# Second layer norm applied by ScalarE, the attention output's remainders by GpSimd, and all engines' orders set anew

## What is computed

```python
x = x + attention(layernorm(x), Wq, Wk, Wv, Wo)
x = x + moe(layernorm(x), ...)
# attention: 16 heads of 16, q and k through elu + 1, causal running sums
kv_sum += k_i (outer) v_i;  k_sum += k_i
out_i = (q_i @ kv_sum) / (q_i . k_sum + 1e-8);  result = out @ Wo.T
# moe: sigmoid router over 8 experts in 4 groups, the best 2 groups,
# the best 4 experts, weights normalised and times 2.5; plus a shared expert
y = sum_e cw_e * ((silu(x @ Wg_e) * (x @ Wu_e)) @ Wd_e)
layernorm(x) = (x - mean) / sqrt(var + 1e-5)
```

## Time and profile before

| what | us |
|---|---|
| median of 3 timed runs | 1055.8 (1051.72 to 1056.35) |
| the profiled execution | 1048.01 |
| its span, first to last instruction | 1046.2 |
| TensorE busy | 978.1 |
| VectorE busy | 832.0 |
| GpSimd busy | 529.2 |
| ScalarE busy | 459.9 |

### The profile page before, as it was taken

The page is one execution under the profiler, slowest core; times in us unless marked ns, Lnnn a source line. Parts: engine busy times, 40 slices in busy tenths (PEclk is TensorE's granted clock), DMA queues, the critical chain, the costliest instruction groups (busy, mean ns, idle before and its releaser), DMA issues. The chain is left out here.

```text
span 1046.2 us, 34557 instructions
## 1 busy us (share of the span) xinstructions
PE 978.1 (93%) x14749; PEld 838.1 (80%) x14749; DVE 832.0 (80%) x1751; ACT 459.9 (44%) x856; POOL 529.2 (51%) x432
## 2 busy tenths in 40 slices
...
GB/s 224 4 21 44 82 64 150 111 84 154 25 174 87 107 133 53 160 70 146 100 68 159 51 175 86 133 106 64 152 67 148 113 77 154 41 149 43 142 76 46
DMA packets 262457, 105.71 MB, mean 101 GB/s; under 512 B 175648, under 2 KB 244768, under 8 KB 262304
## 3 DMA queue, kind: packets, MB, share of 16 engines
...
## 5 line engine op out<-in xcount | busy, mean ns | idle before, releaser
L766 POOL TENSOR_TENSOR et<-et,cw_all 128x512 f32<-128x512 f32 x124 | 162.1, 1315 | 278.9 <-DMA cw_all<-cw_dram 179.8
L1025 PE MATMUL bank<-xt_hi,wg_hi 128*128 128x512 f32 x576 | 238.0, 413 | 11.4 <-DVE compare L880 7.9
L1025 PE MATMUL bank<-xt_lo,wg_hi 128*128 128x512 f32 x576 | 228.8, 397 | 0.0
L1025 PE MATMUL bank<-xt_hi,wg_lo 128*128 128x512 f32 x576 | 228.5, 397 | 0.0
L769 POOL TENSOR_TENSOR h_lo<-et,h_hi 128x512 fp32r<-128x512 f32 x142 | 183.9, 1305 | 74.8 <-ACT h_hi L719 74.8
L719 ACT ACTIVATE h_hi<-et 128x512 fp32r<-128x512 f32 x144 | 89.9, 626 | 177.3 <-POOL et L766 128.0
L1025 PE MATMUL y_bank<-wd_hi,h_hi 128*128 128x256 f32 x576 | 163.5, 284 | 0.1
L1025 PE MATMUL y_bank<-wd_lo,h_hi 128*128 128x256 f32 x576 | 162.7, 282 | 0.0
L1025 PE MATMUL y_bank<-wd_hi,h_lo 128*128 128x256 f32 x576 | 162.2, 282 | 0.0
L710 ACT ACTIVATE et<-bank 128x512 f32<-128x512 f32 x144 | 82.3, 594 | 170.3 <-POOL h_lo L769 95.3
L1025 PEld LDWEIGHTS bank<-xt_hi,wg_hi 128*128 128x128 f32 x576 | 108.8, 189 | 46.4 <-DVE compare L880 9.1
...
## 6 DMA issues: line engine op xcount, KB each, us to landing
...
x_dram<-blocks SPq DMA_DIRECT2D x112, 128.0 KB, 3.5
...
```

The lines of the kernel that those rows point to most:

```text
L766: nc.gpsimd.tensor_tensor(et[:, i % ET, :], et[:, i % ET, :], weights, ALU.mult).then_inc(weighed, 1)
L1025: ins = nc.tensor.matmul(dst, l, r, start=first and n == 0, stop=last and n == 2, skip_group_check=shared)
```

## The change

`ln2_apply` moves from VectorE's list to ScalarE's: four activations with a scale and a bias, `x * rstd2 + shift2`, in place of four `tensor_scalar` instructions. For them VectorE's `ln2_stats` leaves the negative mean, and GpSimd's `rstd2` does a second, small multiply for the bias after its power. All `at` remainders move from VectorE's lists to GpSimd's. The lists of all five engines and the banks are written anew; in `STEP`, `ln1_stats.0.0` now comes ahead of `blocks.1.2` on VectorE, `route.0.2` ahead of `gate.0.2` and `up.0.2`, and `router.0.2` ahead of `gate.0.2` on TensorE. In `FIRST` the warm transposes are 13, 14, 10 and 15 instead of 13, 23, 10, 13 and 10, and the second x is loaded ahead of the second weight piece. Of `FIRST` and `LAST` the diff below shows TensorE's lists, SP's first and ScalarE's last.

```diff
@@ -36,126 +36,127 @@
 STEP = {
     "PE": """
-        up.5.3 wo.0.2 wo.1.2 down.0.3 up.8.3 down.1.3 down.2.3 gate.6.3 state.0.1 gate.8.3 gate.7.3 values.0.1
-        down.3.3 up.6.3 down.4.3 down.5.3 scores.1.1 up.7.3 gate.0.2 values.1.1 router.0.2 up.0.2 down.6.3
-        inter.0.1 inter.1.1 v.1.0 q.0.0 k.0.0 k.1.0 gate.1.2 q.1.0 gate.3.2 gate.2.2 up.1.2 down.7.3 up.2.2
-        down.8.3 scores.0.0 gate.4.2 up.3.2 up.4.2 gate.5.2 v.0.0
+        up.5.3 wo.0.2 wo.1.2 down.0.3 gate.7.3 down.1.3 down.2.3 gate.8.3 state.0.1 up.6.3 gate.6.3 down.3.3
+        values.0.1 up.7.3 down.4.3 scores.1.1 up.8.3 down.5.3 inter.0.1 router.0.2 up.0.2 gate.0.2 gate.1.2
+        up.1.2 down.6.3 gate.2.2 k.0.0 k.1.0 down.7.3 values.1.1 v.1.0 q.0.0 inter.1.1 up.2.2 down.8.3 q.1.0
+        gate.4.2 scores.0.0 gate.3.2 up.4.2 up.3.2 gate.5.2 v.0.0
         """,
     "ACT": """
-        split.3.3 split.5.3 gate.6.3 split.4.3 ln1_apply.0.0 gate.8.3 gate.7.3 take.3.2 wide.1.1 take.2.2
-        split.6.3 gate.0.2 take.0.0 split.8.3 route.0.2 take.1.0 split.0.2 v.1.0 split.7.3 q.0.0 k.0.0 k.1.0
-        at.1.1 q.1.0 gate.3.2 at.0.1 gate.1.2 gate.2.2 q_split.0.0 split.1.2 split.2.2 gate.4.2 q_split.1.0
-        gate.5.2 v.0.0 wide.0.0
+        split.3.3 ln2_apply.0.2 split.5.3 split.4.3 gate.8.3 gate.7.3 gate.6.3 ln1_apply.0.0 split.7.3
+        take.3.2 take.2.2 wide.1.1 split.6.3 route.0.2 gate.0.2 take.0.0 gate.1.2 take.1.0 split.8.3 k.0.0
+        gate.2.2 k.1.0 v.1.0 q.0.0 split.0.2 at.0.1 split.1.2 q_split.0.0 q.1.0 at.1.1 gate.3.2 gate.4.2
+        split.2.2 gate.5.2 q_split.1.0 wide.0.0 v.0.0
         """,
     "POOL": """
-        split.2.3 weigh.4.3 weigh.5.3 weigh.3.3 rstd2.0.2 split.5.3 split.3.3 rstd1.0.0 split.4.3 weigh.6.3
-        take.3.2 take.2.2 weigh.8.3 split.6.3 weigh.7.3 take.0.0 take.1.0 split.8.3 split.7.3 split.0.2
-        weigh.1.2 weigh.2.2 split.1.2 qk.1.0 qk.0.0
+        split.2.3 weigh.4.3 weigh.3.3 weigh.5.3 rstd2.0.2 split.3.3 split.5.3 rstd1.0.0 split.4.3 weigh.7.3
+        weigh.6.3 take.3.2 take.2.2 split.6.3 split.7.3 weigh.8.3 take.0.0 take.1.0 split.8.3 weigh.1.2
+        split.0.2 at.0.1 qk.0.0 weigh.2.2 split.1.2 at.1.1 qk.1.0
         """,
     "DVE": """
-        wo.0.2 wo.1.2 ln2_stats.0.2 ln2_apply.0.2 blocks.1.2 ln1_stats.0.0 state.0.1 gate.6.3 blocks.0.0
-        gate.8.3 up.6.3 gate.7.3 up.8.3 mask.7.1 mask.4.1 mask.5.1 mask.6.1 up.7.3 router.0.2 spread.1.1
-        spread.0.1 gate.0.2 up.0.2 route.0.2 rank0.0.2 mult.0.1 mult.1.1 q.0.0 k.0.0 cum.0.0 k.1.0 rank1.0.2
-        cum.1.0 gate.3.2 q.1.0 gate.1.2 up.1.2 gate.2.2 blocks.2.0 up.2.2 at.1.1 mask.0.0 mask.2.0 mask.1.0
-        result.0.3 up.3.2 den.1.0 gate.4.2 at.0.1 up.4.2 gate.5.2 den.0.0 mask.3.0 up.5.2
+        wo.0.2 wo.1.2 ln2_stats.0.2 ln1_stats.0.0 blocks.1.2 gate.8.3 state.0.1 gate.6.3 gate.7.3 up.6.3
+        up.7.3 blocks.0.0 mask.6.1 up.8.3 mask.7.1 mask.5.1 spread.1.1 router.0.2 mask.4.1 route.0.2 gate.0.2
+        spread.0.1 gate.1.2 up.0.2 up.1.2 rank0.0.2 rank1.0.2 k.0.0 cum.0.0 k.1.0 mult.0.1 cum.1.0 gate.2.2
+        q.0.0 up.2.2 mult.1.1 blocks.2.0 result.0.3 q.1.0 mask.1.0 mask.3.0 mask.0.0 mask.2.0 den.0.0 gate.3.2
+        gate.4.2 up.4.2 gate.5.2 up.3.2 den.1.0 up.5.2
         """,
     "SP": """
-        load_x.0.0 put.1.2 get.1.2 put.0.0 get.0.0 cw_store.0.2 cw_load.0.2 cw_load.3.2 cw_load.1.2 put.2.0
-        cw_load.2.2 cw_load.5.2 get.2.0 store.0.3 cw_load.4.2 cw_load.7.2 cw_load.6.2
+        load_x.0.0 put.1.2 get.1.2 put.0.0 get.0.0 cw_store.0.2 cw_load.0.2 cw_load.1.2 put.2.0 cw_load.5.2
+        cw_load.3.2 store.0.3 cw_load.4.2 cw_load.2.2 get.2.0 cw_load.6.2 cw_load.7.2
         """,
...
 FIRST = {
...
     "PE": """
-        turn.0.0 turn.1.0 warm.13.0 k.0.0 q.0.0 v.0.0 k.1.0 scores.0.0 q.1.0 v.1.0 k_turn.1.0 k_turn.0.0
-        warm.23.0 state.0.0 warm.10.0 scores.1.0 values.0.0 turn.0.1 turn.1.1 inter.0.0 values.1.0 k.0.1
-        inter.1.0 q.0.1 v.1.1 wo.1.0 wo.0.0 k_turn.0.1 q.1.1 k.1.1 warm.13.0 k_turn.1.1 turn.2.0 turn.3.0
-        scores.0.1 warm.10.0 gate.2.0 gate.0.0 gate.1.0 v.0.1 router.0.0 up.0.0 turn.1.2 state.0.1 turn.0.2
-        up.1.0 scores.1.1 values.0.1 k.0.2 inter.0.1 k.1.2 q.0.2 values.1.1 q.1.2 k_turn.0.2 up.2.0 inter.1.1
-        v.0.2 v.1.2 scores.0.2 gate.4.0 gate.3.0 up.4.0 gate.5.0 k_turn.1.2 up.3.0
+        turn.1.0 turn.0.0 warm.13.0 v.0.0 k.0.0 q.0.0 q.1.0 k.1.0 warm.14.0 scores.0.0 k_turn.1.0 v.1.0
+        turn.1.1 k_turn.0.0 values.0.0 turn.0.1 scores.1.0 k.1.1 state.0.0 k.0.1 q.0.1 values.1.0 inter.1.0
+        inter.0.0 q.1.1 k_turn.0.1 v.1.1 wo.1.0 wo.0.0 v.0.1 scores.0.1 warm.10.0 k_turn.1.1 turn.3.0 turn.2.0
+        warm.15.0 state.0.1 router.0.0 turn.1.2 turn.0.2 scores.1.1 values.0.1 k.0.2 gate.2.0 k.1.2 gate.1.0
+        q.0.2 inter.0.1 gate.0.0 values.1.1 up.1.0 up.0.0 v.0.2 inter.1.1 up.2.0 v.1.2 scores.0.2 q.1.2
+        gate.4.0 up.3.0 gate.3.0 k_turn.0.2 up.4.0 k_turn.1.2 gate.5.0
...
     "SP": """
-        load_x.0.0 consts.0.0 piece.0.0 piece.1.0 piece.2.0 piece.3.0 piece.4.0 load_x.0.1 piece.5.0 piece.6.0
-        piece.7.0 piece.8.0 piece.9.0 load_x.0.2 cw_store.0.0 cw_load.3.0 cw_load.0.0 cw_load.1.0 cw_load.2.0
+        load_x.0.0 consts.0.0 piece.0.0 load_x.0.1 piece.1.0 piece.2.0 piece.3.0 piece.4.0 piece.5.0 piece.6.0
+        load_x.0.2 piece.7.0 piece.8.0 piece.9.0 cw_store.0.0 cw_load.3.0 cw_load.1.0 cw_load.0.0 cw_load.2.0
         cw_load.4.0 cw_load.7.0 cw_load.5.0 cw_load.6.0
         """,
...
 LAST = {
     "PE": """
-        down.0.13 up.5.13 wo.0.14 down.1.13 wo.1.14 down.2.13 scores.1.15 down.3.13 gate.6.13 values.0.15
-        up.6.13 gate.8.13 up.8.13 gate.7.13 state.0.15 down.4.13 down.5.13 down.6.13 values.1.15 router.0.14
-        gate.0.14 up.7.13 inter.1.15 up.0.14 gate.1.14 inter.0.15 down.7.13 gate.2.14 up.1.14 up.2.14
-        down.8.13 wo.0.15 gate.3.14 wo.1.15 up.4.14 up.5.14 gate.4.14 gate.5.14 down.0.14 up.3.14 down.1.14
-        down.2.14 gate.6.14 gate.7.14 gate.8.14 up.6.14 down.3.14 up.8.14 down.4.14 router.0.15 up.2.15
-        up.7.14 gate.2.15 up.1.15 up.0.15 down.5.14 gate.0.15 gate.1.15 down.6.14 down.7.14 down.8.14
-        gate.3.15 up.4.15 gate.4.15 up.5.15 up.3.15 down.0.15 down.1.15 gate.5.15 gate.6.15 down.2.15 up.6.15
-        gate.8.15 down.3.15 up.7.15 gate.7.15 up.8.15 down.4.15 down.5.15 down.6.15 down.7.15 down.8.15
+        wo.0.14 up.5.13 wo.1.14 gate.6.13 down.0.13 down.1.13 gate.7.13 state.0.15 down.2.13 gate.8.13 up.6.13
+        down.3.13 up.7.13 down.4.13 up.8.13 values.0.15 scores.1.15 down.5.13 router.0.14 inter.0.15 gate.0.14
+        up.0.14 down.6.13 values.1.15 down.7.13 up.1.14 gate.2.14 inter.1.15 down.8.13 up.2.14 gate.3.14
+        gate.1.14 wo.1.15 wo.0.15 gate.5.14 gate.6.14 up.4.14 up.5.14 down.0.14 up.3.14 down.1.14 down.2.14
+        gate.4.14 gate.8.14 down.3.14 up.6.14 gate.7.14 up.7.14 up.8.14 router.0.15 gate.2.15 gate.0.15
+        up.1.15 down.4.14 down.5.14 up.0.15 gate.1.15 up.3.15 down.6.14 down.7.14 gate.5.15 down.8.14 up.2.15
+        gate.3.15 up.4.15 gate.4.15 gate.8.15 down.0.15 down.1.15 up.5.15 gate.7.15 down.2.15 gate.6.15
+        up.7.15 up.6.15 down.3.15 down.4.15 up.8.15 down.5.15 down.6.15 down.7.15 down.8.15
...
     "ACT": """
-        split.3.13 gate.6.13 split.4.13 split.6.13 split.5.13 wide.1.15 gate.8.13 take.2.14 take.3.14
-        gate.7.13 route.0.14 at.1.15 split.7.13 gate.1.14 gate.0.14 split.8.13 gate.2.14 at.0.15 split.0.14
-        split.2.14 gate.3.14 split.1.14 gate.4.14 gate.5.14 split.3.14 split.5.14 split.4.14 gate.7.14
-        take.3.15 take.2.15 gate.6.14 gate.8.14 route.0.15 split.6.14 split.8.14 gate.0.15 split.7.14
-        gate.1.15 gate.2.15 split.0.15 split.1.15 split.2.15 gate.4.15 gate.3.15 gate.5.15 split.3.15
-        split.5.15 split.4.15 gate.6.15 gate.7.15 gate.8.15 split.6.15 split.7.15 split.8.15
+        split.3.13 split.4.13 wide.1.15 ln2_apply.0.14 split.5.13 gate.8.13 gate.6.13 gate.7.13 split.7.13
+        take.3.14 take.2.14 split.6.13 split.8.13 gate.0.14 route.0.14 gate.2.14 at.0.15 split.0.14 at.1.15
+        gate.1.14 gate.3.14 split.2.14 split.1.14 gate.5.14 ln2_apply.0.15 split.3.14 split.5.14 gate.4.14
+        split.4.14 gate.6.14 gate.8.14 take.3.15 take.2.15 gate.7.14 route.0.15 split.7.14 split.6.14
+        gate.0.15 split.8.14 gate.1.15 gate.2.15 split.1.15 split.0.15 gate.3.15 gate.4.15 split.2.15
+        gate.5.15 split.4.15 split.3.15 gate.7.15 split.5.15 gate.6.15 split.6.15 split.7.15 gate.8.15
+        split.8.15
...
 BANK = {
-    ("gate", 0): 2, ("gate", 1): 0, ("gate", 2): 1, ("gate", 3): 2, ("gate", 4): 5, ("gate", 5): 3, ("gate", 6): 5,
-    ("gate", 7): 4, ("gate", 8): 1, ("k", 0): 5, ("k", 1): 1, ("k_turn", 0): 4, ("k_turn", 1): 2, ("o", 0): 3,
-    ("o", 1): 0, ("q", 0): 2, ("q", 1): 5, ("router", 0): 1, ("scores", 0): 3, ("scores", 1): 0, ("scores", 2): 4,
-    ("scores", 3): 2, ("scores", 4): 0, ("scores", 5): 1, ("scores", 6): 4, ("scores", 7): 2, ("state", 0): 0,
```

(51 more changed lines are left out.)

64 lines of the change are left out of this document (31 added, 33 removed).

## The result

| | before | after |
|---|---|---|
| median of the timed runs, us | 1054.6 (4 runs) | 1079.8 (4 runs, 1079.17 to 1080.44) |
| ratio, 95% interval | 1 | 1.0242 (1.0215 to 1.0268) |
| span of the profiled execution, us | 1046.2 | 1078.0 |
| mean granted clock | 0.993 | 0.966 |
| state product to state product, mean of 12 steps | 62.6 | 64.2 |

The change made the kernel 2.4% slower, 25 us; 2% faster had been forecast. (Among the runs of all kernels here one of 1171 and one of 1367 us had a mean granted clock of 0.753 and 0.635 and one of 2346 us the full clock; no ratio uses them, and the trace of run 11, which is that of 1367 us, is not read.) First the page of the changed kernel: busy times as in the earlier trace rows, and the granted clock in the 40 slices, in tenths.

A forecast was written before the change was run, and what follows sets the result against it. TensorE, 93% busy, was taken as the bound, so only its waits could be won: 59.2 + 1.0 + 0.5 + 0.3 = 61.0 us a step, 21 us less in all, 1027, plus 7.8 carried over: 1035 us, range 1010 to 1062.

The forecast's parts named there:

- The floor: TensorE's steady step without any wait: 59.2 us, against 62.6 before the change.
- The two waits that were to go: TensorE's loop waits for the up bank ahead of scores.1.1 (16.0 us) and for the state sums (7.9 us).
- The x load: Load of x ahead of ln1_stats: lands 5.0 us after issue in the median, 3.9 to 9.7.
- The router due at 26.4: Router product on TensorE, due 26.4 us after the start of up.5.3 in the new step.
- k.0.0: Product on TensorE, forecast to wait 0.4 to 0.5 us for up.1.2's bank, behind the routing on VectorE.
- the sign that the forecast is wrong: Stated signs: scores.1.1 still waits, the router waits over 2.5 us, or VectorE doesn't idle before ln1_stats.
- a wait of 0.9 to 1.0 us: TensorE's router product waiting for xt_lo, ready at 27.3 us but wanted at 26.4, each step.
- the last chain: From the end of blocks to xt_lo, taken as 13.4 us from the trace before the change.
- The bounds of the forecast's row: Range of the router wait: none with x landing after 3.9 us, 2.5 us with x after 6.5.
- Head and end: Outside the loop: nothing at the end, within 2 us; 3 us either way at the start.
- Late x, slower: Rival, 0.15: ln1_stats behind the x load; slower once waits pass 3.4 us a step, landing 6.6 us or more.
- VectorE held by GpSimd: Rival, 0.05: GpSimd's added 2.6 us falls wholly on the routing chain ahead of k.0.0; step 63.6 us, 1069 us.

The follow-up runs named there:

- run 11: The kernel of run 1 with the second weight piece loaded ahead of the x of batch 1 at the start: 1037.8 us, 0.9868.
- run 1: The changed kernel with blocks.1.2 put ahead of ln1_stats.0.0 in VectorE's steady list: 1034.5 us, 0.9833 to the kernel before.
- run 3: The kernel before with only the remainders of the attention's output moved to GpSimd, just ahead of weigh.1.2: 1072.8 us, 1.0196.

## Why the prediction was wrong

**What held.** The floor: 59.2 us without waits; the changed kernel's step without a wait took 59.4. The two waits that were to go are gone. The new step up to `wo` and ln2_stats: 5.1 and 7.6 us forecast, 444.05 - 438.94 = 5.1 and 446.58 - 438.94 = 7.6 measured. The activation (2.1 us a step, 33.3 us over 64 beside the earlier trace rows) and the small multiply (0.20 us) cost what they were given. The x load: 5.0 us in the median as before, none over 6.5. The router due at 26.4: 469.25 - 3.93 - 438.94 = 26.4. k.0.0 did not wait. The place of the new wait was named, and so was the sign that the forecast is wrong: a router wait over 2.5 us.

**Step that failed, first half: the size of "a wait of 0.9 to 1.0 us".** It measured 2.9 to 4.7 us in eight of twelve steps. In the step shown xt_lo is ready at 30.2 and not 27.3, 2.9 us late, in two terms. (a) ln1_stats ends at 13.9 instead of 12.6: the load was issued at 5.7 instead of 5.2, VectorE saw it 5.25 us later instead of 5.0, and GpSimd held `m_sum` 0.5 us, a hold that the forecast looked for in another place only, and there with a chance of 0.05.

(b) "From the end of blocks to xt_lo the last chain takes 13.4 us". Here it was 15.0 us (454.13 to 469.10), of which 6.05 from put to get and 5.7 from the get to its landing. The row was not a poor sample of the kernel before: in its loop the same chain takes 12.5 to 13.7 us in twelve of thirteen steps (15.0 in one). It grew under the change, to 12.6 to 15.9 us with a median of 14.2. What grew most is the landing of the get: 3.9 to 4.2 us in eleven of the thirteen steps before and 3.9 to 4.1 in all of run 1, but 4.6 to 6.0 in those eleven steps of the changed kernel in which `put.0` (461.55 in the rows of SP) goes out at most 1.4 us behind it, and 3.9 and 4.1 in the two in which it comes 1.8 and 2.8 us behind; in run 1 it comes 3.3 us behind or later. So late blocks bring the get beside the next four writes. That alone does not do it, since before `put.0` stood 1.34 us behind the get in five steps with landings of 4.1 to 4.2; what does was not tried apart. Run 1 has a chain of 14.0 us all the same, the landing shorter and the takes behind it later, but its blocks start 2.6 us sooner against the state product.

The bounds of the forecast's row moved the x load alone; the chain behind it, a longer term, had no range.

**Second half: the clock was left out.** I had counted 1.6 us of slow matmuls behind a 1.6 us wait at 327.79 as something to win in the floor, and put none behind the new waits. Between the third and the fifteenth state product they came to about 19 us, against 5.5 before. The Trainium skill (TensorE: Matmul & The Clock Gate, "HAM oscillation — how this bites in real kernels") tells of a kernel whose TensorE waited some 3 to 5 us for a transfer in each tile and began every next tile at the low clock; the trace agrees, with 1.1 to 2.6 us of slow matmuls behind each wait of 2.9 to 4.7. The account of a step: 59.4 + 41.4/13 of waits + 19/12 of clock = 64.2 us, as measured, against the 61.0 forecast. That it closes to a tenth is partly luck: the count of slow matmuls leaves out the router product (up to 0.75 us longer) and holds 0.2 us a step that are in the 59.4 already.

**Head and end.** Forecast 0, within 3 and 2. The third state product came 4.9 us later (129.94 against 125.08); run 1 keeps 3.7 of it, so it belongs to the new lists of the start. From state.0.14 to the end 177.2 us against 169.9. Run 1 has 170.6, so 6.6 of the 7.3 us go with the one placement: 4.3 in the steady step that this stretch begins with (63.35 us from its state product to the next against 59.05) and 2.3 behind it. With 12 x 1.63 of the loop the three make 19.6 + 4.9 + 7.3 = 31.8 us, the difference of the two spans.

**The rivals.** "Late x, slower" named the mechanism and tied it to the wrong condition, a landing of 6.6 us or more: none was, and it came true at 5.0, since the 2.9 us were spent elsewhere (0.5 on the issue, 0.25 on seeing the landing, 0.5 on `m_sum`, 1.6 on the chain); its 3.4 us of waits as the turning point were about right (3.2 a step measured), but only the clock behind them carried it past. "VectorE held by GpSimd", given 0.05, decided nothing here by the moved work (0.6 us a step came of the place of the statistics), but did in run 3 (+20 us): the position it depends on is one entry of a list. Busy times went down 51 on VectorE (60 forecast), up 31 on GpSimd (39) and up 28 on ScalarE (33).

Undoing the one placement gives the 1035 us of the forecast; part of that agreement is luck, since the medians here lay only 4 to 5 us above the profiled execution of before, not 7.8. By differences it is -18 us against -21.
